# Weighted sums of values in column tiles of TensorE: 32 stationary columns for each head instead of 9

## What is computed

```
x = x + tanh(g_xattn[0]) * xattn0(layernorm(x), ctx)       # softmax over all 1601 keys
x = x + tanh(g_ffn[0])   * moe0(layernorm(x))              # 8 experts, top 2
x = x + tanh(g_xattn[1]) * xattn1(layernorm(x), ctx)       # softmax over the 32 best keys only
x = x + tanh(g_ffn[1])   * l1(layernorm(x))                # self attention (256 keys) + 8 experts, top 2

# each attention, for a head:
w   = softmax(q @ k.T * scale)          # [queries, keys]
out = w @ v                             # the step that is changed
```

## Time and profile before

| | |
|---|---|
| median of 3 runs | 6209.23 us (6196.12 to 6210.12) |
| the profiled execution | 6214.0 us |
| its span, first to last instruction | 6212.0 us |
| mean granted TensorE clock | 0.918 of 2.4 GHz |
| TensorE matmuls busy | 4855.6 us, 78% (34758 records) |
| TensorE weight loads busy | 2301.8 us, 37% |
| VectorE busy | 4696.6 us, 76% |
| ScalarE busy | 4011.8 us, 65% |
| GpSimd (POOL) busy | 867.1 us, 14% |

### The profile page before, as it was taken

The page is one execution under the profiler, slowest core; times in us unless marked ns, Lnnn a source line. Parts: engine busy times, 40 slices in busy tenths (PEclk is TensorE's granted clock), DMA queues, the critical chain, the costliest instruction groups (busy, mean ns, idle before and its releaser), DMA issues. The chain is left out here.

```text
span 6212.0 us, 109517 instructions
## 1 busy us (share of the span) xinstructions
PE 4855.6 (78%) x34758; PEld 2301.8 (37%) x34758; DVE 4696.6 (76%) x23731; ACT 4011.8 (65%) x5196; POOL 867.1 (14%) x1650
## 2 busy tenths in 40 slices
PE   4878678888777888688788878887788788878676
PEld 2424234343433434243343434334343343434222
DVE  3476987869788686877868687787878868686872
ACT  1447656767575676676667676775767567676663
POOL 4111111111111111111111111111111111010000
PEclk7879989999898999899899999998999899999887
DMA  4222212222122222222222222221222222121110
GB/s 106 65 68 52 59 42 53 67 48 63 43 62 48 52 63 55 60 47 54 60 49 61 50 64 53 55 65 42 63 50 63 51 46 63 33 60 25 31 29 17
DMA packets 356330, 332.18 MB, mean 53 GB/s; under 512 B 102074, under 2 KB 313149, under 8 KB 355711
## 3 DMA queue, kind: packets, MB, share of 16 engines
q1 hardware_dynamic: 355710, 324.84, 22.4%
HBM read 217.54 MB, written 107.13 MB: 52 GB/s over the span
## 5 line engine op out<-in xcount | busy, mean ns | idle before, releaser
L958 DVE MAX8 cand<-s 128x8 f32<-128x67 f32 (+1 forms) x12288 | 2107.7, 214 | 29.9 <-DVEq L1110 18.0
L930 ACT ACTIVATE prob<-wide 128x1024 f32<-128x1024 f32 (+1 forms) x1792 | 1771.5, 1027 | 432.6 <-PE wide L652 232.2
L1056 DVE TENSOR_REDUCE part<-score 128x1 f32<-128x512 f32 (+1 forms) x2048 | 1151.0, 565 | 837.3 <-PE score L611 651.1
L911 ACT ACTIVATE s<-wide 128x1024 f32<-128x1024 f32 (+1 forms) x1024 | 857.1, 844 | 729.0 <-PE wide L626 431.2
L652 PE MATMUL wide<-q,k_att 128*128 128x256 bf16 (+1 forms) x6656 | 995.0, 283 | 180.2 <-ACT prob L930 88.1
L698 PE MATMUL att<-prob,v 128*9 128x256 f32 (+1 forms) x14336 | 1073.2, 399 | 60.8 <-ACT u L941 32.6
L920 ACT ACTIVATE below<-wide 128x1024 bf16<-128x1024 f32 (+1 forms) x832 | 809.8, 1023 | 276.6 <-PE wide L652 272.4
L611 PE MATMUL score<-k_scan,q 128*128 128x512 bf16 (+1 forms) x2048 | 710.2, 354 | 321.6 <-DVE part L1056 300.8
L674 PE MATMUL wide<-below,minus_ident 128*128 128x512 bf16 (+1 forms) x1664 | 512.4, 391 | 416.5 <-ACT below L920 416.2
L652 PEld LDWEIGHTS wide<-q,k_att 128*128 128x128 bf16 (+1 forms) x6656 | 594.1, 102 | 625.0 <-ACT prob L930 222.6
L626 PE MATMUL wide<-k_scan,q 128*128 128x512 bf16 (+1 forms) x2048 | 562.5, 360 | 139.2 <-ACT prob L930 70.3
(11 more groups left out here) (165 smaller groups left out, 5660.0 us busy)
## 6 DMA issues: line engine op xcount, KB each, us to landing
k_scan<-k_stack SPq DMA_DIRECT2D x512, 150.1 KB, 3.2
k_stack<-split_b SPq DMA_DIRECT2D x576, 128.0 KB, 2.5
k_att<-k_stack SPq DMA_DIRECT2D x384, 192.0 KB, 3.4
ctxT<-in_ctx_dram SPq DMA_DIRECT2D x32, 800.5 KB, 5.5
q_stack<-split_b SPq DMA_DIRECT2D x192, 64.0 KB, 2.1
q<-q_stack SPq DMA_DIRECT2D x128, 96.0 KB
self_stack<-split_b SPq DMA_DIRECT2D x192, 64.0 KB, 2.1
k_self<-self_stack SPq DMA_DIRECT2D x64, 96.0 KB
```

The costliest lines, as they stand in the source:

```text
L911: scalar.activation(m.s[tile % 4][:, a0:a0 + wd], ps[:, 0:wd], ACT.Copy).then_inc(sem["wide_done"], 1)
L930: scalar.activation(pr[0:kc, :], ps[0:kc, :], ACT.Exp, scale=SCALE).then_inc(sem["wide_done"], 1)
L958: i = vector.max(cand[:, c, :], s[:, KCUT[c]:KCUT[c + 1]])
L1056: vector.tensor_reduce(m.part[:, QT * hh + qt, c:c + 1], score[i % 2][:, 0:wd], AX.X, ALU.max).then_inc(sem["score_max"], 1)
```

## The change

Each value buffer gets 24 further columns at its end and is also held as a flat array, so that a slice of 32 columns can start at any head. The summing step takes 32 columns from the head's first one: its own nine and the 23 that follow, which are the next heads' values and ones, for the last heads those of the next chunk or the 24 columns of 1.0 at the end. It writes 32 partitions of `att` for each head. The wait for the values' write names the fourth write of the batch for every chunk. The fills on POOL cover the longer buffers. What is read from `att` afterwards stays the same.

```diff
@@ buffers
-        m.v = [[sb(f"v{l}_{n}", [P, NC, H, HD + 1]) for n in range(2)] for l in range(2)]
-        m.v2 = sb("v2", [P, QT, H, HD + 1])
+
+        WIDTH = H * (HD + 1)
+        m.v_flat = [[sb(f"v{l}_{n}", [P, NC * WIDTH + 24]) for n in range(2)] for l in range(2)]
+        m.v2_flat = sb("v2", [P, QT * WIDTH + 24])
+
+        def by_head(x):
+            return x[:, 0:(x.shape[1] - 24)].rearrange("p (c h j) -> p c h j", h=H, j=HD + 1)
+        m.v, m.v2 = [[by_head(x) for x in xs] for xs in m.v_flat], by_head(m.v2_flat)
@@ the summing step
-                            kc, end, v = chunk(NK, c), c == NC - 1, m.v[l][b % 2]
-                            q.wait_ge(sem["wide_done"], after("w_v_out", l, b, c // 4))
+                            kc, end, v = chunk(NK, c), c == NC - 1, m.v_flat[l][b % 2]
+                            q.wait_ge(sem["wide_done"], after("w_v_out", l, b, 3))
                             q.wait_ge(sem["wide_done"], after("exp_%d" % l, g, c))
...
-                            kc, end, v = P, c == QT - 1, m.v2
+                            kc, end, v = P, c == QT - 1, m.v2_flat
...
                         for j in range(HG):
-                            r = tensor.matmul(att[32 * j:32 * j + HD + 1, 0:S], v[0:kc, c, j0 * HG + j, :],
+                            v0 = c * WIDTH + (j0 * HG + j) * (HD + 1)
+                            r = tensor.matmul(att[32 * j:32 * j + 32, 0:S], v[0:kc, v0:v0 + 32],
                                               m.prob[n % 3][0:kc, j * S:(j + 1) * S], start=(c == 0), stop=end,
                                               tile_position=(0, 32 * j), skip_group_check=True)
@@ POOL, at the start
-                    gpsimd.memset(m.v[0][n][:, :, :, :], 1.0).then_inc(filled, 1)
+                    gpsimd.memset(m.v_flat[0][n][:, :], 1.0).then_inc(filled, 1)
...
-                    gpsimd.memset(m.v[1][n][:, :, :, :], 1.0).then_inc(filled, 1)
-                gpsimd.memset(m.v2[:, :, :, :], 1.0).then_inc(filled, 1)
+                    gpsimd.memset(m.v_flat[1][n][:, :], 1.0).then_inc(filled, 1)
+                gpsimd.memset(m.v2_flat[:, :], 1.0).then_inc(filled, 1)
```

## The result

The changed kernel takes 6234.03 us (8 runs, 6221.67 to 6248.58), the kernel before 6209.04 us beside it (8 runs, 6185.63 to 6213.01): a ratio of 1.0051, 95% interval 1.0035 to 1.0067. A later measurement of the same two gave 6239.35 to 6210.87 us, ratio 1.0038 (1.0024 to 1.0052). The medians differ by 25 and by 28 us, and the two intervals together reach from 15 to 42 us. I call it some 25 us. I had forecast 6218 with a range of 6190 to 6250: the range held it, the forecast is 16 us short, and instead of the +8.7 us of my sum the kernels differ by some 25. "Slower by over 0.3%" had a chance of 0.23 from me, "within 0.3%" 0.67.

What follows compares the result with a forecast made beforehand. TensorE, VectorE and ScalarE, coupled by short waits, bound the kernel, none alone. 6214.0 us plus 8.7 for the wider load, 0 for the rest, gave 6222.7; less 4.8 to the median, 6218, range 6190 to 6250.

Steps and rivals of the forecast that it cites:

- my sum: Whole kernel: 6214.0 us for the profiled execution plus 8.7 us for the wider load, 6222.7; all other parts 0.
- Part 1, the load: Summing step's loads: 32 columns take 111 ns, 20 more, exposed once per run of groups; 20.3 us on TensorE.
- My 1015 heads: Times the summing step's weight load begins after idle, each exposing one load's extra 20 ns.
- My term of 8.7: Wider load's cost at the end: 20.3 us on TensorE times a reach of 0.43; bounds 0 and 20.3.
- The rival of loads in series: At group heads: four column tiles share one load path, 81 us on TensorE, 35 at the end, median 6244; chance 0.14.
- Parts 2, 3 and 4: Wider result in the accumulator, changed wait for the values, longer value buffers: cost 0 each, the result within 2 us.
- The clock: TensorE's granted clock, 0.918 on average: nothing in the trace ties it to nine columns; stays at 0.92 within 0.01.
- rival (c): TensorE's granted clock rises with wider tiles: 0.025 won everywhere would be 1.4%, some 88 us, median 6121; chance 0.05.
- the 88 us: Gain over the whole run if TensorE's granted clock rose by 0.025 everywhere, 1.4% of the time.
- phase: With no cost of its own the change makes the three engines meet otherwise, up to 20 us either way; chance 0.10.
- Part 4: Longer value buffers, POOL fills and shifted addresses cost 0; small phase shifts worth up to 5 us in a batch.
- My own sign of being wrong: The prediction falls if the batches change by more than 5 us while the loads behave as told.

Runs made afterwards that it cites:

- second series: The changed kernel with 32 columns measured once more beside the kernel before: 6239.35 us to 6210.87, ratio 1.0038.
- first filler kernels: 704 unread matmuls where TensorE waits for ScalarE, added to the kernel before: 6169.37 us, ratio 0.9929; to the changed kernel: 6181.46 us, ratio 0.9949.
- tiny matmul: Kernel before plus a matmul of one moving column at the head of each summing step: 6240.82 us to 6207.18, ratio 1.0057.
- second pair of fillers: 768 further unread matmuls in stage 0 besides the 704: kernel before with both 6241.04 us, ratio 1.0054; changed kernel with both 6265.28 us, ratio 1.0095.
- bare pause: Kernel before plus an already satisfied wait ahead of each summing step's four matmuls: 6214.64 us to 6205.75, ratio 1.0020.

## Why the prediction was right or wrong

**Part 1, the load, was right in its mechanism and somewhat low in its size.** 111 ns expected, 112 measured; eight loads beside one another; the growth exposed once for each run of steps. My 1015 heads came from the list of waits, which holds 1006 of them now; by the matmuls 1115 runs are longer by 20 ns and 162 by some 7. The price on TensorE is so 24 us at a clock that is not lower (1081.3 - 1057.5), not 20, and with the lower clock of the changed kernel 29. The transposes, which I had said would stay, went from 301 to 307 ns, where 9 columns in the new layout have 304; the copy of u stayed.

What of it reached the end is known less well. Taken at a like clock, 32 columns cost more than 9 by 25.3 - 13.7 = 12 us (changed kernel, the mean of its second series, less 3.8 us x 3.6 for its clock), by 11 to 17 us between the first filler kernels and by 6 us between the second. The reach of the tiny matmul, 0.55 to 0.6, would make 13 to 14 us of the 24. My term of 8.7 lies inside these 6 to 17 us; most of them point to some 12, a reach of 0.5.

**The rival of loads in series was wrong,** as the rows had said: the sixteen loads spread over 0.59 us under 1.07 us of matmuls, and the step grew by 0.02 us, not by 0.08. The Trainium skill's rule ("TensorE: Matmul & The Clock Gate", Part 3, The mechanism), that loads overlap with running matmuls only where the row group differs, is contradicted by these rows too: all four tiles have the same row groups, and their loads overlap with each other's matmuls at 9 and at 32 columns. The same section of the Trainium skill also has loads pulled ahead where they target the background weight buffer, and no run here tells that from the effect of different column tiles. The loads of L658 (L652 before) use all 128 columns of the array, and eight of them (0.78 us) lie under eight of its matmuls (1.04 us) as well, so different column tiles are not needed for an overlap.

**Parts 2, 3 and 4 were right about their costs.** The copy of u stays at 385 ns, and layout, fills and wait together cost nothing (ratio 0.9994).

**The clock was the step that failed.** I had weighed it only as a gain, and had written that it would stay at 0.92 within 0.01. It did: 0.9135 to 0.9137 against 0.917. But my own rival (c) held a price and I never multiplied it with a small loss. That price had a slip in it: the two batches differ by 0.03 of clock and 5 us of 351, which is 2.9 us for each 0.001 over the run, where I had set the 88 us against 0.025. The runs show 3.6 to 4.4. At 3.8 the loss of 0.0036 is 14 us, as much as the delay itself. The rows had shown it: the same pair of batches, 351 us at 0.98 and 356 at 0.95, I read as clock in rival (c) and as phase in Part 4, and left it in the range. My own sign of being wrong came about too: the place of the 351 us batch takes 359 us in the changed kernel while the loads behave as told, and I had named 5 us.

So a sum that fits is some 12 us of delay and 14 us of clock, together 26. It is less exact than it looks: the 12 us of the second series are what is left after the clock's part is taken off, and by the other pairs the delay is anything from 6 to 17 us, so the clock's part is 8 to 19 of the 25.

That the measured 6234 us lies inside the range is partly luck. The upper end of 6250 was there for loads in series and for phase, and neither came: the loads run beside one another, and the new layout with 9 columns costs nothing (0.9994).

What stays open is how a delay of some 20 ns at 1277 places costs 0.004 of clock. With wider loads the clock fell in three widths and between the second pair of fillers; with a bare pause it fell by half as much, 2.4 times its standard error; with a tiny matmul at the same heads and with the first fillers it did not fall. By these runs neither the width alone nor the delay alone decides it. It may be a matter of how the marginal stretches fall in time, which no run here tested. The price of a lost 0.001 is shown; the amount lost is only measured for each kernel.

## What to carry to other kernels

Read the granted clock of every run beside its time, and price a small loss as well as a large gain: here 0.001 was worth some 4 us of 6200, and about half of the cost of the change went that way. A load that is longer by 20 ns costs once for each run of tiled steps, not for each load, and some half of it reached the end where three engines wait for each other. Where TensorE waits anyway, a matmul that nobody reads can pay for itself through the clock (0.7 to 0.8% here); where no wait covers it, the same matmul costs more than it brings.

## What the runs showed of the hardware

Fillers of the same duration and at the same places raised the mean granted clock from 0.917 to 0.927 when they worked on 128 partitions and not at all (0.918) when they worked on 8. Loads of fp32 weights took 91, 101, 107 and 112 ns at 9, 20, 26 and 32 columns, 0.91 ns a column, and loads of four column tiles ran beside one another at each width: eight were over in 119, 137, 148 and 158 ns. The 23 columns from 9 to 32 made a single step of the kernel longer by 20 ns at 2.4 GHz and by 39 ns at 1.2 GHz (medians). A matmul of one moving column in front of a step delayed it by about 0.03 us.
